# Placement of final copies, ring refills and residual sums in an eight-image convolution and attention kernel on one core

## What is computed

```python
x = x + _L0_conv_ref(_gn(x), ...)
x = x + _L1_conv_ref(_gn(x), ...)

# L0: four depthwise filters of 7 taps (row, column, both diagonals), a softmax weight per
# channel and direction, the weighted sum of the four, and a full 3x3 convolution
feats = jnp.stack([feat_h, feat_v, feat_d45, feat_d135], axis=1)
context = jnp.mean(feats * feats, axis=(3, 4)).reshape(x.shape[0], -1)
hid = jax.nn.leaky_relu(context @ w_att1.T, negative_slope=0.2)
attn = jax.nn.softmax((hid @ w_att2.T).reshape(x.shape[0], 4, DIM), axis=1)[..., None, None]
feat_geom = jnp.sum(attn * feats, axis=1)
return lax.conv_general_dilated(feat_geom, w_proj, (1, 1), ((1, 1), (1, 1)), ...)

# L1: linear attention, a second attention whose queries pass through an FFT, a pointwise
# layer, GELU and an inverse FFT, a depthwise 3x3 convolution, and a projection
attnf = jax.nn.softmax(jnp.einsum('bhdn,bhen->bhde', qf, k) * temperature, axis=-1)
outf = jnp.einsum('bhde,bhen->bhdn', attnf, vf).reshape(b, c, h, w)
return conv1x1(outf, w_projf)
```

## Time and profile before

| | |
|---|---|
| median of 3 runs | 4011.15 us (4006.11 to 4013.85) |
| profiled execution, own time | 4010.97 us |
| its span | 4009.3 us |
| PE busy | 3374.3 us, 84% |
| DVE busy | 2954.0 us, 74% |
| ACT busy | 1791.1 us, 45% |
| POOL busy | 694.5 us, 17% |
| DMA moved | 440.70 MB, mean 110 GB/s |
| granted PE clock, mean | 0.922 of 2.4 GHz |

### The profile page before, as it was taken

How to read it: one execution, slowest core, us unless ns; L and a number is a source line. 1 busy time by engine, 2 the same in 40 slices (tenths; PEclk the granted TensorE clock), 3 DMA queues, 4 the chain that set the end, 5 groups by cost and what they waited for, 6 DMA issues and landing times.

```text
span 4009.3 us, 56727 instructions
## 1 busy us (share of the span) xinstructions
PE 3374.3 (84%) x20626; PEld 2713.3 (68%) x20626; DVE 2954.0 (74%) x2721; ACT 1791.1 (45%) x2921; POOL 694.5 (17%) x1336
## 2 busy tenths in 40 slices
PE   4648998699976999679986899869997799968998
PEld 2336687568765687666875677756876668757787
DVE  6976987579865998569984698758986599844211
ACT  5423682238623384135831467223861348410550
POOL 1013003220132102230022200322013200223003
PEclk9768999799998999889997999979998899989999
DMA  4367224943259324692338622494235923376004
GB/s 105 94 145 179 64 74 84 212 120 79 70 103 234 80 74 90 133 214 62 74 80 181 165 65 74 92 225 113 68 83 109 221 78 78 78 146 151 1 11 86
DMA packets 210824, 440.70 MB, mean 110 GB/s; under 512 B 125696, under 2 KB 125936, under 8 KB 210512
## 3 DMA queue, kind: packets, MB, share of 16 engines
q1 hardware_dynamic: 141392, 255.36, 26.3%
q0 software_dynamic: 69120, 181.32, 21.3%
HBM read 189.27 MB, written 150.99 MB: 85 GB/s over the span
## 4 chain that ended last, share of the span: by engine, by line
PE 31%; DVE 31%; issue 24%; DMA 10%; ACT 2%; POOL 1%; DVEq 0%; SPq 0%; ACTq 0%; POOLq 0%
DVE feat L806 22%; DMA feat<-feats_d 8%; PE banks L1083 6%; PE banks L1064 4%; PE banks L1069 4%; PE banks L1093 3%; PE banks L1151 3%; PE banks L1113 2%; PE banks L1099 2%; PE banks L1100 2%; DVE acc L938 2%; DVE feat L938 2%; DVE x L896 1%; PE banks L1073 1%; DMA shifted<-e_hi 1%
## 5 line engine op out<-in xcount | busy, mean ns | idle before, releaser
L806 DVE SCALAR_TENSOR_TENSOR feat<-xin,w,feat 96x1536 f32<-96x1536 f32 x540 | 947.0, 1807 | 1.8
L1064 PE MATMUL banks<-e_hi,wp 128*96 128x384 f32 x1728 | 397.5, 382 | 356.2 <-DMA shifted<-e_hi 240.5
L1064 PEld LDWEIGHTS banks<-e_hi,wp 128*96 128x96 f32 x1728 | 314.2, 186 | 408.0 <-issue 243.5
L585 ACT ACTIVATE squares<-feat 96x1536 bf16<-96x1536 f32 x192 | 285.1, 1485 | 589.2 <-DVE feat L806 587.0
L806 DVE SCALAR_TENSOR_TENSOR feat<-xin,wh,feat 96x1536 f32<-96x1536 f32 x288 | 520.3, 1807 | 30.1 <-ACT feat L573 28.4
L806 DVE SCALAR_TENSOR_TENSOR feat<-xin,wv,feat 96x1536 f32<-96x1536 f32 x288 | 520.3, 1807 | 0.0
L1064 PE MATMUL banks<-e_hi,a 128*96 128x384 f32 x1728 | 360.9, 356 | 106.7 <-ACT res L651 106.0
L1064 PEld LDWEIGHTS banks<-e_hi,a 128*96 128x96 f32 x1728 | 289.8, 170 | 149.5 <-ACT res L651 96.7
L1069 PE MATMUL banks<-e_lo,wp 128*96 128x384 f32 (+1 forms) x1728 | 369.7, 363 | 0.0
L1069 PE MATMUL banks<-e_lo,a 128*96 128x384 f32 (+1 forms) x1728 | 350.4, 349 | 0.0
L1069 PEld LDWEIGHTS banks<-e_lo,wp 128*96 128x96 f32 x1728 | 310.2, 180 | 32.6
(11 more groups left out here) (161 smaller groups left out, 5456.3 us busy)
## 6 DMA issues: line engine op xcount, KB each, us to landing
feats_d<-feat SPq DMA_DIRECT2D x160, 576.0 KB, 4.1
feat<-feats_d SPq DMA_DIRECT2D x160, 576.0 KB, 8.4
shifted<-e_hi POOLq DMA_DIRECT2D x576, 97.2 KB, 2.7
feat<-in_x SPq DMA_DIRECT2D x48, 576.0 KB, 9.5
res<-in_x POOLq DMA_DIRECT2D x96, 288.0 KB, 4.7
out<-x POOLq DMA_DIRECT2D x96, 288.0 KB, 2.9
out<-res POOLq DMA_DIRECT2D x96, 288.0 KB, 4.4
xin<-in_x SPq DMA_DIRECT2D x32, 792.0 KB, 8.7
```

What stands on the lines that cost most here:

```text
L585: act.activation(squares[0 if first_image(b) or u <= LEAD else 1][:], feat[:, d], ACT.Square, accum_out=sq[:, d, ch:ch + 1]).then_inc(squa ...
L806: dve.scalar_tensor_tensor(out=dst, in0=src, scalar=taps_w[d](k), in1=dst, op0=ALU.mult, op1=ALU.add).then_inc(tap_done, 1)
L1064: pe.matmul(dst, w1[:, t, :], rows(e_hi, a0, n, dx, 128), start=(t == CENTRE_FIRST[0]), stop=False)
```

## The change

It has four parts.

1. **Final copies.** The final copies of the attention convolution that ACT does before unit work 9, 10 and 11 and after it are 3, 4, 3 and 1 (with the twelfth, 2) in place of 2, 2, 2 and 5.
2. **Ring and spare copies.** `fill` is parted in `shift` (three ring DMAs) and `copy` (two spare DMAs), each on semaphores of its own. For group j POOL first issues the ring's three, then the spare copies of group j + 1; those of group 0 (and of group 1 with it, in the attention convolution) are issued at the start. PE waits for both semaphores.
3. **Residual sums.** `SUMS_AFTER` becomes (0, 0, 1, 2, 1, 2), and `start` does three more before the norm, so GN_AT is 9: nine of twelve sums stand ahead of the next image's norm, one behind it, and two in its first taps.
4. **Splits.** The hooks for `e_split` come after taps 1, 2, 4, 5, 7, 8, 10 and 11 of a unit.

```diff
-SUMS_AFTER = (0, 0, 0, 1, 1, 1)
-GN_AT = sum(SUMS_AFTER) + 2
+SUMS_AFTER = (0, 0, 1, 2, 1, 2)
+GN_AT = sum(SUMS_AFTER) + 3
+COPIES_AFTER = (3, 7, 10)
...
-FILL_DMAS = 5
+RING_DMAS, BULK_DMAS = 3, 2
...
-            def fill(sems, j):
+            def shift(sems, j):
+
+                for g in range(3):
+                    at = (j * GR + g) * EP
+                    pool.dma_start(shifted[g * SPARE:(g + 1) * SPARE, j % 2, :], e_hi[2 * SPARE:C, at:at + SHIFTED])\
+                        .then_inc(sems[j % FILLS], 16)
+
+            def copy(sems, j):
...
                 pool.dma_start(e_hi[C:C + SPARE, lo:hi], e_hi[0:SPARE, lo:hi]).then_inc(done, 16)
                 pool.dma_start(e_lo[C:C + SPARE, lo:hi], e_hi[SPARE:2 * SPARE, lo:hi]).then_inc(done, 16)
-                for g in range(3):
...
-                pool.wait_ge(e_hi_ready, i * U_E + min(U_E, (j + 1) * GR // TR + 1))
-                apart(pool)
-                fill(e_filled, j)
+                e_rows(i, j)
+                shift(e_shifted, j)
+                for n in range(0 if j == 0 else j + 1, min(NG, j + 2)):
+                    e_rows(i, n)
+                    copy(e_copied, n)
...
-                fill(fg_filled, j)
+                fg_rows(b, j)
+                shift(fg_shifted, j)
+                if j == 0:
+                    copy(fg_copied, 0)
+                if j >= 1:
+                    for n in range(1 if j == 1 else j + 1, min(NG, j + 2)):
+                        fg_rows(b, n)
+                        copy(fg_copied, n)
...
                 for u in range(LEAD + 1, UNITS):
-                    copies(j, j + 2)
-                    j += 2
+                    copies(j, COPIES_AFTER[u - LEAD - 1])
+                    j = COPIES_AFTER[u - LEAD - 1]
...
-                between()
-                between()
+                for _ in range(GN_AT - sum(SUMS_AFTER)):
+                    between()
...
-                        taps(b, u, hooks=[(n, split) for n in range(2, TAPS // 2 + 1, 2)])
+                        taps(b, u, hooks=[(n, split) for n in (1, 2, 4, 5, 7, 8, 10, 11)])
...
-                        pe.wait_ge(*filled(fg_filled, b, j))
+                        pe.wait_ge(*filled(fg_shifted, b, j, RING_DMAS))
+                        pe.wait_ge(*filled(fg_copied, b, j, BULK_DMAS))
```

More of the change, by code:

```diff
@@ L256, in build @@
         fin_ready, fin_copied = sem("fin_ready"), sem("fin_copied")
-        fg_filled = [sem(f"fg_filled{n}") for n in range(FILLS)]
-        e_filled = [sem(f"e_filled{n}") for n in range(FILLS)]
+        fg_shifted, fg_copied = ([sem(f"{k}{n}") for n in range(FILLS)] for k in ("fg_shifted", "fg_copied"))
+        e_shifted, e_copied = ([sem(f"{k}{n}") for n in range(FILLS)] for k in ("e_shifted", "e_copied"))
         waits_passed = {e.engine: sem(n) for e, n in (
@@ L281, in shifted_rows, with filled @@
             return shifted[:, j % 2, at:at + TR * EP].rearrange("p (r c) -> p r c", c=EP)[:, :, 0:W]
-        def filled(sems, i, j):
-            return sems[j % FILLS], (i * (NG // FILLS) + j // FILLS + 1) * FILL_DMAS * 16
+        def filled(sems, i, j, dmas):
+            return sems[j % FILLS], (i * (NG // FILLS) + j // FILLS + 1) * dmas * 16
         def small_chain(eng, s, total, i):
@@ L432, in fill, with e_rows, fg_rows @@
                 pool.dma_start(e_lo[C:C + SPARE, lo:hi], e_hi[SPARE:2 * SPARE, lo:hi]).then_inc(done, 16)
-                for g in range(3):
-                    at = (j * GR + g) * EP
-                    pool.dma_start(shifted[g * SPARE:(g + 1) * SPARE, j % 2, :], e_hi[2 * SPARE:C, at:at + SHIFTED])\
-                        .then_inc(done, 16)
+            def e_rows(i, j):
+                pool.wait_ge(e_hi_ready, i * U_E + min(U_E, (j + 1) * GR // TR + 1))
+                apart(pool)
+            def fg_rows(b, j):
+                pool.wait_ge(fg_hi, b * NCH + min(NCH, (j + 1) * GR // CR + 1))
+                apart(pool)
             def fill_e(i, j):
@@ L453, in fill_fg @@
                 apart(pool)
-                pool.wait_ge(fg_hi, b * NCH + min(NCH, (j + 1) * GR // CR + 1))
-                apart(pool)
-                fill(fg_filled, j)
+                fg_rows(b, j)
[6 more added lines that the diff above has]
+                        copy(fg_copied, n)
             def start(b):
@@ L1175, in ready @@
                 def ready(j):
-                    pe.wait_ge(*filled(e_filled, i, j))
+                    pe.wait_ge(*filled(e_shifted, i, j, RING_DMAS))
+                    pe.wait_ge(*filled(e_copied, i, j, BULK_DMAS))
                     pe.wait_ge(e_ready, i * U_E + min(U_E, (j + 1) * GR // TR + 1))
```

## The result

| | before | after |
|---|---|---|
| median | 4010.16 us (4006.11 to 4013.85, 4 runs) | 3984.22 us (3983.31 to 3985.79, 4 runs) |
| ratio after / before | | 0.9936, 95% interval 0.9919 to 0.9953 |
| span of the profiled execution | 4009.3 us | 3983.2 us |
| mean granted clock | 0.922 | 0.921 |

The change makes the kernel 26 us faster, where 64 were forecast; the time lies inside the range given. From its page first the span and the chain of work that ended last; the earlier trace rows had PE and DVE at 31% each.

A forecast was written before the change was run, and what follows sets the result against it. No engine alone bounds it: DVE waits for PE's late attention convolution, then full DMA and the norm. Passes 1 to 6 -45.6, pass 0 +13.2, pass 7 -31.3, pass 8 0: -63.7, 3947 us; range 3907 to 3991, 8 in 10 3875 to 4018.

The forecast's parts named there:

- Part 1, -20.8 us in seven passes: Attention convolution: with the final copies moved, group 11 starts 20.8 us earlier in each of passes 1 to 7.
- 7.6 us back behind the norm: DVE behind the next image's norm: two sums instead of six, 1.91 us each, 7.6 us less.
- The norm 20.8 us later: Next image's norm: its group sums come 20.8 us later against the products, held until group 9 ends.
- The rule 7y - 209: Total time change in us for a norm delay y, less what pass 7 changes; crosses zero at y = 30.
- the budget: DMA behind the products: 26.89 MB at 244 GB/s take 110.2 us before group 9's ring third has landed.
- Pass 0, +13.2: Pass without attention convolution: norm 20.8 us later, 7.6 us back, so 13.2 us longer.
- Pass 7, -31.3: Pass without a next image: convolution end 10.5 us earlier by the byte sum, with part 1 31.3 us less.
- The share of the DMA engines: DMA from 1668 to 1764: busy share 1.07 at 244 GB/s, read as engines full.
- the first rival: L0 convolution not held by DMA, only by placement: y = 7.7, about 3852 us; chance 0.23.
- Not held by DMA: The first rival: only placement holds the convolution, y = 7.7, about 3852 us; chance 0.23.
- norm too late: POOL's ring before groups 6 to 9 delays the norm, y = 31.2, 4027 us, slower; chance 0.17.
- Gains cancel: Copy 3 late, group 5 stalls: part 1 brings some 12 us, not 20.8; 4009 us; chance 0.08.

The follow-up runs named there:

- the old refills: The changed kernel with one refill of five transfers per group again and the old splits, copies and sums as changed: 3951.82 us, ratio 0.9854.
- sums alone: The kernel before with only SUMS_AFTER and GN_AT changed, copies, refills and splits as before: 4099.84 us.
- the copies alone: The kernel before with only the final copies moved (3, 4, 3, 1 and 1), sums, refills and splits as before: 3874 us.
- thin stores: The changed kernel with each store writing one row of eight (96 of 768 columns), the rest of the output left out: 3969.29 us, ratio 0.9889.

## Why the prediction was right or wrong

- **Part 1, -20.8 us in seven passes: right.** Start to P fell by 20.5 us in passes 1 to 6. DVE's wait is 3.55 us where about 4 was forecast, and no wait of PE for ACT's copies is left.
- **7.6 us back behind the norm: right.** 59.9 to 52.3.
- **The norm 20.8 us later: the term that failed.** It came 25.9 us later. The rule 7y - 209 gives -28 us for it, so the whole miss (-26 against -64) is this one size. The step that failed is the budget itself: that the norm waits until POOL's 10.04 MB and SP's 16.85 MB are through, the ring's third of group 9 last. In the change that third lands at P + 118.1 (forecast 114.5), but PE waits for it only 0.3 us in the mean; the last long wait for the ring stands ahead of group 7, 5.0 to 6.2 us in passes 1 to 6, and behind it the groups run at their own pace. The sentence that names the error is the one on the refills: "it is inside the budget, since bytes and not order set the time". Order and slots set it: at equal bytes the norm stands 4.9 us earlier with the old refills, 8.3 earlier with a third slot, and 3.8 earlier with only the place of a wait changed, while 2.66 MB less gave 1.5 us. That the budget gave 20.8 where sums alone measured 21.1 is an agreement of numbers, so luck. The rate in it was sound: over the 96 us of the earlier trace rows the kernel before moved 244 GB/s and the kernels with early sums and all their stores 242 to 255 (means of passes 1 to 6). What is refuted is that the sum of the bytes sets the norm; it matters which of them are wanted first, and when they are asked for. The spare copies fetched a group ahead, priced at "1 us of issue", belong to the same step: half of the 4.9 us is theirs.
- **Two readings of rows.** The 240.5 us of waits for the ring were put down to the stretch where the engines are full; 163 of them stand at groups 0 and 1, where PE waits for the first products and the copies of them. And 16.85 MB are SP's from 1660 to 1770, not from 1668 to 1764; that changes nothing in the sum, since it is all that SP loads there.
- **Pass 0, +13.2:** +17.3, by the same term. **Pass 7, -31.3:** -30.1; its convolution gave 7.7 of the 10.5, part 1 22.4.
- **The share of the DMA engines** was read as a limit at 244 GB/s. The rule of the Trainium skill weighed against it (DMA: Bandwidth & Descriptors, Specifications, about 358 GB/s) would have given the first rival's 3852; the kernel moved 230 GB/s over 110 us there and did not come near that time. So the trace's rate was the better guide, though the bytes were not what the norm waited for.
- **Rivals.** "Not held by DMA" needed y = 7.7, "norm too late" from 30 on: neither. The latter named the right place, POOL's ring in front of groups 6 to 9: the longest wait stands ahead of group 7. "Gains cancel" (part 1 at 12 us) is out.
- **What the forecast held and did not say:** its own terms give -145.6 for the copies and +82 for the rest. Measured: -141 for the copies alone and +115 for the rest, of which the sums are 103 on top of the refills. The best part of the change was alone the better change.

The landing of a ring copy is the size that the forecast did not price. The trace has 2.9 us in the median over the whole run and 8.5 in the stretch; this row is from the page of the change:

```profile
shifted<-e_hi POOLq DMA_DIRECT2D x576, 97.2 KB, 2.9
```

The Trainium skill, DMA: Bandwidth & Descriptors, Anatomy of one DMA, gives about 2.0 us and the bytes at 436 GB/s, an estimate of 2.2 us for this copy. The median over the run, 2.9 us, agrees roughly; that of the busy stretch is nearly four times the estimate, and it was the busy one that counted.

## What to carry to other kernels

Cost each part of a change by itself: two that pull in opposite directions can hide a large gain (here 141 us, of which 115 were lost again). Where a buffer has two slots, compare the landing time in the busy stretch, not the bytes, with the work of the one slot that covers it; and before giving it a third, ask whose loads the earlier traffic will displace. A consumer in program order (a norm behind nine sums) makes everything ahead of it critical, so move it as far forward as its own operands allow, and no further.

## What the runs showed of the hardware

- A DMA share of 1.00 went with 210 GB/s (thin stores, 110 us), 1.04 with 272 and 1.19 with 269 (the change, 7 and 5.9 us). The share alone did not tell the rate. Over 96 us with all stores it was 243 to 249 GB/s at shares of 1.07 to 1.10, in the windows shown.
- A pause of PE of 5.81 us was followed by 5.9 us at a granted clock of 0.50, which made the group 2.8 us longer. Behind the pause of 3.96 us ahead of group 3 nine matmuls took 3.19 us too; behind those of 2.59 and 3.33 us they took 1.84 and 1.83.
- Two queues that wanted the engines at once slowed each other: SP's share fell by 4.1 points when POOL's refills came earlier, and the last product moved from P + 75.2 to P + 78.4.
- A 97.2 KB copy within SBUF landed in 2.9 us in the median of the run and in 8.5 us while both queues were busy.
